# A graph layer on one core: edge tiles of 128 in blocks of 24, and a wait ahead of every eight gathers

## What is computed

```python
h = relu(layernorm(x))
m_in = concat([h[src], edge_attr])                    # 400000 x 192
messages = relu(m_in @ msg_w1 + msg_b1) @ msg_w2 + msg_b2
aggregated = segment_sum(messages, dst)               # 12500 x 128
out = x + relu(concat([h, aggregated]) @ upd_w1 + upd_b1) @ upd_w2 + upd_b2
```

## Time and profile before

| | |
|---|---|
| median of 3 runs | 4913.87 us (4913.0 to 4914.27) |
| profiled execution, own time | 4917.07 us |
| its span, first to last instruction | 4915.3 us |
| mean granted clock of TensorE | 0.608 of full speed |
| gathers, early and from the table | 75 and 3125 |

### The profile page before, as it was taken

How to read it: one execution, slowest core, us unless ns; L and a number is a source line. 1 busy time by engine, 2 the same in 40 slices (tenths; PEclk the granted TensorE clock), 3 DMA queues, 4 the chain that set the end, 5 groups by cost and what they waited for, 6 DMA issues and landing times.

```text
span 4915.3 us, 59369 instructions
## 1 busy us (share of the span) xinstructions
PE 3511.1 (71%) x16139; PEld 3183.0 (65%) x16139; DVE 2248.7 (46%) x3651; ACT 595.7 (12%) x887; POOL 3881.7 (79%) x3208
## 2 busy tenths in 40 slices
PE   5677777777677767766777677767776677767766
PEld 3666666666666666666666666666666666666666
DVE  5455555555444444444444444444444444444444
ACT  5111111111100000001010001000100010001002
POOL 7777777777778787877777777777777777777774
PEclk8666666666655555556555655655565655565566
DMA  7322222222222222222222222222222222222223
GB/s 174 73 67 64 69 66 67 68 66 67 64 64 64 65 65 64 64 64 64 64 66 64 64 64 65 64 64 64 65 65 64 64 64 66 64 64 64 65 64 87
DMA packets 398534, 336.04 MB, mean 68 GB/s; under 512 B 287275, under 2 KB 304299, under 8 KB 397263
## 3 DMA queue, kind: packets, MB, share of 16 engines
q0 software_dynamic: 256000, 208.52, 18.0%
q1 hardware_dynamic: 141810, 126.99, 10.5%
q10 hardware_dynamic: 706, 0.33, 0.0%
HBM read 319.26 MB, written 12.81 MB: 68 GB/s over the span
## 4 chain that ended last, share of the span: by engine, by line
POOL 72%; issue 23%; PE 2%; SPq 1%; DMA 1%; POOLq 0%; DVE 0%; another core or an unknown queue 0%; ACT 0%; ACTq 0%; DVEq 0%
POOL rows L380 72%; SPq L281 1%; PE pre L542 0%; POOLq L374 0%; PE seg L403 0%; DMA rows<-table,index 0%; PE pre L407 0%; PE pre L395 0%; POOLq L378 0%; DMA table<-space 0%; PE seg L467 0%; DMA b_upd_col<-in_b_upd 0%; DVE space L716 0%; PE iota_ps L542 0%
## 5 line engine op out<-in xcount | busy, mean ns | idle before, releaser
L380 POOL DMA_INDIRECT rows<-table,index x3125 | 3789.7, 1213 | 953.9 <-issue 953.0
L467 PE MATMUL seg<-space,hidden 125*128 125x128 f32 x6400 | 1517.1, 420 | 1030.1 <-ACT hidden L613 697.5
L467 PEld LDWEIGHTS seg<-space,hidden 125*128 125x128 f32 x6400 | 1353.0, 316 | 1166.2 <-issue 640.8
L785 DVE TENSOR_TENSOR hidden<-pre,rows 125x640 f32<-125x640 f32 x625 | 514.9, 824 | 1826.4 <-DMA rows<-table,index 1614.0
L433 PE MATMUL pre<-w_attr_sb,attr_space 64*125 64x128 f32 x6250 | 1304.0, 384 | 15.1 <-issue 15.1
L433 PEld LDWEIGHTS pre<-w_attr_sb,attr_space 64*125 64x125 f32 x6250 | 1173.1, 284 | 116.1 <-issue 103.7
L613 ACT ACTIVATE hidden<-hidden 125x640 f32<-125x640 f32 x640 | 471.5, 737 | 4247.4 <-DVE hidden L785 3476.0
L834 DVE TENSOR_REDUCE part_space<-space 125x128 f32<-125x640 f32 x640 | 790.6, 1235 | 0.0
L826 DVE TENSOR_TENSOR space<-iota_ps,dst_rel 125x640 f32<-125x640 f32 x640 | 526.0, 822 | 118.3 <-DVE part_space L834 71.1
L476 PE MATMUL seg<-part_space,w_msg_t_sb 128*128 128x128 f32 x1280 | 393.4, 407 | 224.8 <-DVE part_space L834 208.4
L476 PEld LDWEIGHTS seg<-part_space,w_msg_t_sb 128*128 128x128 f32 x1280 | 319.8, 306 | 258.7 <-issue 258.5
(11 more groups left out here) (65 smaller groups left out, 503.9 us busy)
## 6 DMA issues: line engine op xcount, KB each, us to landing
attr_space<-in_attr SPq DMA_DIRECT2D x640, 156.2 KB
rows<-table,index POOLq DMA_INDIRECT x3125
index<-in_src SPq DMA_DIRECT2D x625, 2.4 KB
table<-space SPq DMA_DIRECT2D x25, 224.0 KB
out<-x_all SPq DMA_DIRECT2D x4, 1120.0 KB
x_all<-in_x SPq DMA_DIRECT2D x2, 1120.0 KB
x_all<-in_x SPq DMA_DIRECT2D x1, 2240.0 KB
attr_space<-in_dst_rows SPq DMA_DIRECT2D x2, 781.2 KB
```

Of the source, the lines that this page charges most:

```text
L380: pool.indirect_dma_start(rows[0:EDGES, k, t, :], None, table, bass.IndirectOffsetOnAxis(index[:, k, t:t + 1], 0))\
L467: last = pe.matmul(seg[:, 0, 0:WINDOW], hidden[0:EDGES, hidden_slot(k), t * D:(t + 1) * D], mask[:, k % 2, t, :], start=(t == 0), stop=(t ...
L785: dve.tensor_tensor(hidden[0:EDGES, k, :], pre[0:EDGES, k % 2, 0:TILES * D], rows[0:EDGES, k].rearrange("p t d -> p (t d)"), ALU.add).then ...
```

## The change

The same computation with another cut of the edges and another order. New sizes:

```diff
-EDGES = 125
+EDGES = 128
 UNROLL = 5
-TILES = 5
-CHUNK = TILES * EDGES
-WINDOW = 128
+PAIR = 8
+PAIRS = 3
+TILES_B = PAIRS * PAIR
+SLOTS = 8
+AHEAD = 5
+WINDOW = 80
-EARLY = 15
+EARLY = 3
```

```diff
+            def gather(source, j, tiles):
+                for t in tiles:
+                    pool.indirect_dma_start(slot_rows(j)[:, t, :], None, source, bass.IndirectOffsetOnAxis(index[0:EDGES, j, t:t + 1], 0))\
+                        .then_inc(gathered[j][t // PAIR], 16)
...
+                need(pool, hidden_summed, b - (SLOTS - 1))
+                for q in range(pairs_of(b)):
+                    before_i, before_j, before_q = (i, j, q - 1) if q else (*behind(i, j, 1), PAIRS - 1)
+                    pool.wait_ge(gathered[before_j][before_q], before_i * (16 * PAIR) + 16 * PAIR)
+                    pool.sem_inc(pool_turns, 1)
+                    gather(table, j, range(q * PAIR, q * PAIR + tiles_of(b, q)))
```

- The attributes of two tiles stand one above the other on 128 partitions, and the weights are block-diagonal, so that one product of 256 columns serves two tiles:

```diff
-        w_attr_sb = sb("w_attr_sb", [2 * K_ATTR, D])
+        w_attr_sb = sb("w_attr_sb", [2 * K_ATTR, 2 * D])
...
+            def attr_product(i, j, q, two, stop):
+                start = q * COLUMNS + two * EDGES
+                return pe.matmul(columns(j, q, PAIR)[:, two * 2 * D:(two + 1) * 2 * D], attrs[:, j % 2, start:start + EDGES],
+                                 w_attr_sb[:, :], start=True, stop=stop)
```

More of the change, by code:

```diff
@@ L308, in _ @@
[L308 to L321, removed]
-                    sp.dma_start(attrs[:, k, :], attr[bass.ds(c, 1)].rearrange("a f e -> f (a e)"))\
-                        .then_inc(attr_loaded[k], 16)
@@ new lines, in load_block @@
+            def load_block(i, j):
+                b = block_of(i, j)
+                nxt = ahead(i, j, AHEAD)
+                if exists(*nxt) and not (isinstance(b, int) and b + AHEAD < SLOTS):
+                    need(sp, summed, b * PAIRS + (PAIRS - (SLOTS - AHEAD) * PAIRS))
+                    load_index(*nxt)
+                load_attr(i, j)
+            sp.wait_ge(update_ready, after(GROUPS - 1))
+            for j in range(SLOTS):
+                load_block(0, j)
+            with sp.Fori(1, ROUNDS) as i:
+                for j in range(SLOTS):
+                    load_block(i, j)
@@ L384, in _ @@
+            with pool.Fori(1, ROUNDS) as i:
+                for j in range(SLOTS):
+                    gather_block(i, j)
+            for i in range(ROUNDS, -(-(LAST + 1) // SLOTS)):
+                for j in rounds_of(i):
+                    gather_block(i, j)
         @block.tensor
@@ new lines, in update_sums @@
+            def update_sums(i, j):
+                if not exists(i, j):
+                    return
+                b = block_of(i, j)
+                width = pairs_of(b) * WINDOW
+                pe.wait_ge(part_copied, b + 1)
+                pe.wait_ge(mask_sums_made, b + 1)
+                need(pe, accumulated, b * PAIRS)
+                finished = sum(1 for at in FINISH.values() if isinstance(b, int) and at < b + (2 if b < LAST - 2 else 3))
+                need(pe, o_made, finished)
+                pe.matmul(spare[:, 0:width], w_both[:, :], part[:, j % 2, 0:width], start=True, stop=False)
+                pe.matmul(spare[:, 0:width], bias_both[0:EDGES, :], mask_sum[:, j % 2, 0:width], start=False, stop=True)\
+                    .then_inc(seg_ready, 1)
@@ new lines, in finish_group, with finish_groups @@
+            def finish_group(g):
+                pe.wait_ge(u_relued, g + 1)
+                need(pe, o_made, g)
+                for r in range(ROWS):
+                    last = pe.matmul(spare[0:NP, r * D:(r + 1) * D], u[:, r, :], w_upd2_sb[:, :], start=True, stop=True)
+                last.then_inc(o_ready, 1)
+            def finish_groups(i, j):
+                b = block_of(i, j)
+                for g, at in FINISH.items():
+                    if isinstance(b, int) and at == b:
+                        pe.wait_ge(accumulated, (b - 1) * PAIRS)
+                        finish_group(g)
@@ new lines, in edge_block @@
+            def edge_block(i, j, wide):
+                for q in range(pairs_of(block_of(i, j))):
+                    if wide:
+                        attr_products(i, j, q)
+                        wide_sums(i, j, q)
+                    else:
+                        nxt = (i, j, q + 2) if q == 0 else (*ahead(i, j), q - 1)
+                        if exists(*nxt) and nxt[2] < pairs_of(block_of(*nxt[:2])):
+                            attr_products(*nxt)
+                        if q == 0:
+                            update_sums(*behind(i, j, 2))
+                        hidden_sums(i, j, q)
+                if not wide:
+                    finish_groups(i, j)
@@ new lines, in copy_sums, with accumulate @@
+            def copy_sums(i, j):
+                if not exists(i, j):
+                    return
+                b = block_of(i, j)
+                width = pairs_of(b) * WINDOW
+                dve.wait_ge(hidden_summed, b + 1)
+                need(dve, seg_ready, b - 1)
+                dve.tensor_copy(part[:, j % 2, 0:width], seg[:, j % 2, 0:width]).then_inc(part_copied, 1)
+            sites = itertools.count()
+            def accumulate(i, j):
+                if not exists(i, j):
+                    return
+                b = block_of(i, j)
+                site = next(sites)
+                registers = [dve.alloc_register(f"base{c}_of_{site}") for c in range(pairs_of(b))]
+                dve.load(registers, base_row[0:1, bass.ds(b * BASES, pairs_of(b))])
+                for c in range(pairs_of(b)):
+                    base = bass.RuntimeValue.of_register_unchecked(registers[c], min_val=0, max_val=N - 1)
+                    if c == 0:
+                        dve.wait_ge(seg_ready, b + 1)
+                    need(dve, accumulated, b * PAIRS + c)
+                    place = update[:, bass.ds(base, WINDOW)]
+                    dve.tensor_tensor(place, spare[:, c * WINDOW:(c + 1) * WINDOW], place, ALU.add).then_inc(accumulated, 1)
@@ new lines, in edge_loops @@
+                one = divmod(LAST - 1, SLOTS)
+                two = divmod(LAST, SLOTS)
+                make_masks(*one)
+                for q in range(PAIRS):
+                    if q < PAIRS - 1:
+                        sum_rows(*one, q)
+                    if q == 0:
+                        sum_masks(*behind(*one, 1))
+                        copy_sums(*behind(*one, 1))
+                        accumulate(*behind(*one, 2))
+                    if q == 1:
+                        finish_groups(*one)
@@ new lines, in edge_loops @@
+                make_masks(*two)
+                sum_masks(*one)
+                sum_rows(*one, PAIRS - 1)
+                for q in range(PAIRS_LAST):
+                    sum_rows(*two, q)
+                accumulate(*behind(*one, 1))
+                copy_sums(*one)
+                sum_masks(*two)
+                copy_sums(*two)
+                accumulate(*one)
+                accumulate(*two)
+                dve.wait_ge(accumulated, LAST * PAIRS + PAIRS_LAST)
+                for g in REST:
+                    finish_group(g)
```

923 lines of the change are left out of this document (548 added, 375 removed).

## The result

The changed kernel took 4806.73 us (median of 4 runs, 4806.21 to 4807.37), beside 4914.07 for the kernel before: a ratio of 0.9782, with a 95% interval of [0.9765, 0.9799]. Forecast were 4682 us, a gain of 4.7%; measured were 2.2%. The profiled execution took 4807.37 us for a span of 4805.6.

What follows compares the result with a forecast made beforehand. Bound: the number of GpSimd gathers times their beat. Sum: 126 us start + 4530 for 381 groups of eight + 8 for the last five gathers + 19.5 tail = 4683 span, 4682 us as run time; range 4250 to 5550.

Steps and rivals of the forecast that it cites:

- Fewer, wider gathers: Gathers go from 3200 to 3125, 128 rows on 16 engines; descriptor pairs each from 416 to 144.
- g: A gather's work on GpSimd, 1.21 us before; taken as 1.00, bounds 0.50 and 1.24.
- Rival A: A gather's work on GpSimd stays at 1.21 us, so the kernel is slower, 5315 to 5545 us; chance 0.28.
- Rival D: A gather's work follows its descriptor pairs, 0.85 us or less, giving 4225 us; chance 0.20.
- D: Time from a gather's end on GpSimd to its landing, 2.15 us before; taken as 1.55.
- Rival C: The time from work's end to landing stays 2.15 us, giving 4911 us, no change; chance 0.07.
- r: Time from a landing to GpSimd's next gather start; taken as 0.17 us, upper end 0.90.
- Rival B: GpSimd restarts from idle, 0.90 us from landing to next start, giving 4960 us; chance 0.10.
- Rival E: GpSimd's wait costs nothing because the landing is already past, giving 4150 us; chance 0.03.
- The start: Early gathers and node stage ahead of the first table gather: 126 us, range 117 to 140.
- P: Cost of one group of eight table gathers including the wait for the eighth's landing: 11.89 us.
- The tail: From the last gather's landing to the end, with one output group left: 19.5 us, 45.2 before.

Runs made afterwards that it cites:

- run 1: The changed kernel without GpSimd's wait for the eight gathers before, all else kept: 3941.71 us, ratio 0.8015 against the kernel before.
- run 8: The changed kernel with the wait moved behind the first gather of each group: 4373.77 us, ratio 0.8899 against the kernel before.
- run 2: The kernel before with only the constant EDGES changed from 125 to 128 rows a gather, no wait: 3985.25 us, ratio 0.8102.
- run 6: The changed kernel with EDGES back at 125 rows a gather, wait and all else kept: 5962.18 us, ratio 1.2133 against the kernel before.
- run 3: The changed kernel with the wait kept, but for the group before the previous one: 3939.93 us, ratio 0.8012 against the kernel before.
- run 5: The changed kernel again, not edited, in two later jobs: 4734.48 and 4732.80 us, ratios 0.9634 and 0.963 against the kernel before.

## Why the prediction was right and where it was wrong

**The bound, right.** The kernel is still set by what one group of eight gathers costs on GpSimd; TensorE and VectorE stayed covered, busy for 52% and 30%, and even in run 1, for 62% and 37%. In run 8, where the chain is whole, it has 42% GpSimd, 32% issue and 23% DMA.

**Fewer, wider gathers, right.** 3125 gathers, 32 packets each. That these are 144 descriptor pairs on 16 engines remains an inference from the packets. The trace agrees on both shapes with the rule on the number of engines that the prediction quotes from the Trainium skill (DMA: Bandwidth & Descriptors, "Why a DMA increments its semaphore by 16 and not by 1"). Runs 2 and 6 switch between 32 and 80 packets by the constant alone.

**g, nearly right, and in part by luck.** Taken 1.00 (0.50 to 1.24), measured 0.944. The 1.00 was a choice between two bounds, not worked out from a row. That this term alone could turn the sign was true: Rival A, with 1.21, would have been slower, and run 6 measured such a kernel at +21%. Rival D, with g following the pairs (0.85 or less), fell. Only two shapes were measured, and they differ in rows, pairs and engines at once; which of these g follows isn't shown. One reading behind the split of 1.21 into 0.12 and 1.09 was too wide: in the kernel before, the L910 operations that began 0.05 us or more before a gather's start and ran on for 0.14 or more after it held it, but those that began from 0.02 before to 0.05 after it left it at 1.21, though they too covered its first 0.12.

**D, right.** Taken 1.55, measured 1.59; taking off the whole 0.60 of engine time was about right. With 125 rows the landing comes 3.33 - 1.21 = 2.12 after the work's end, close to the 2.15 of the earlier trace rows, so 0.53 were gained. Rival C, which kept 2.15, fell. A few single landings at 128 rows still took as long, this one 3.06 from the start:

```profile
4206.31 3.06 DMA rows<-table,index
```

The Trainium skill (DMA: Bandwidth & Descriptors, "Anatomy of one DMA") has a fixed part of about 2.0 us that scales with nothing. The traces do not agree with that: from start to landing a gather of 125 rows takes 3.33 us and one of 128 rows, with more bytes, 2.54.

**r, wrong.** This is the step that failed: "I take 0.17, from the loop that stays the loop". r measured 0.79, the size of Rival B's 0.90. The row behind the choice was misread. This is the timeline of the kernel before around it, and 14 us later:

```profile
795.84 1.21 POOL L380 DMA_INDIRECT rows<-table,index  x1 [0.30 <-issue]
797.36 1.21 POOL L380 DMA_INDIRECT rows<-table,index  x1 [0.30 <-DMA index<-in_src]
...
810.99 1.21 POOL L380 DMA_INDIRECT rows<-table,index  x1 [0.30 <-issue]
```

The index load landed at 797.19 and the queue's entry behind it followed at 797.21. But this is the 91st of 625 such entries, one ahead of each five gathers, so its own gather is the 451st from the table. Only 441 had started by then; the 451st is the one at 810.99. The gather at 797.36 had been issued before, and began after the usual 0.30 behind the one that ended at 797.05. So the 0.17 lies between two things that don't depend on each other: GpSimd's queue was nine gathers ahead here, and twelve at 497 of the 625 entries. The row at 126.08 was the only one with nothing queued, and its 0.88 was set aside as "code run for the first time". In terms of a group: the beats came out 0.43 lower than taken (7 x (1.31 - 1.248)), the last gather's work 0.06 lower, D 0.04 higher, r 0.62 to 0.65 higher: together the 0.20 between 12.09 and 11.89, or 77 us. The beats are lower because g is, so it was the error of g that hid much of the error of r: r alone is some 240 us (0.62 x 381). Rival B had r nearly right, and its 4960 was too high mostly because its g was 1.00. The prediction's own sign of being wrong came true, too: it named gaps of over 2.2 us ahead of every eighth gather, and they are 3.354 - 0.944 = 2.41, not 1.7. Of the 125 us by which the time was missed, the group has 77 and the start, below, 45.

**Rival E, wrong as a rival, right as a hint.** A wait that ends while gathers are still queued costs nothing: run 3. The prediction priced the wait well enough to be on the right side, but it reckoned the change as one sum. Taken apart, the change is a gain of some 975 us (run 1) and a loss of 793 (run 5 against run 1). Nothing that the runs show needs the wait where it stands. (The chances for a faster kernel add up to 0.585, not 0.57; nothing hangs on it.)

**The start, wrong for the recorded result, too cautious otherwise.** Forecast 126 (117 to 140), measured 171 there and 102 in both repeats, since the new node stage was done earlier. The shorter early gathers alone don't do it: in run 2, with the old node stage, they end at 98.05 and the first table gather starts at 124.97. With 102 and the measured P the sum is 4683 + 77 - 24 = 4736, against 4734 and 4733. The tail was nearly right: forecast 19.5 behind the last landing, measured 19.7 - 2.54 = 17.2.

## What to carry to other kernels

In this kernel GpSimd, waiting for the landing of what it had just issued, paid the landing and its own restart each time, 2.08 us; the same wait set one group back, with six gathers still queued when it ended, cost nothing. Price such a wait by a row in which the engine really stood still: if the idle time ahead of the row is the usual gap, the row says nothing about a restart. And before a landing is put beside the next start, count whether the two belong together; the chain of a profile joins what lies close in time. Before shapes are tuned, try the constants: of the 20% that were to be had here, 19 came from 128 rows a gather, a multiple of 16, in place of 125.

## What the hardware showed that was not expected

- GpSimd's work for an indirect gather of rows of 512 B was 1.21 us for 125 rows in 80 packets and 0.944 for 128 rows in 32 packets. More rows, less time.
- GpSimd's queue ran up to twelve gathers ahead of GpSimd where no wait held it (at 368 of 382 entries in run 1, 497 of 625 in the kernel before), and was six ahead at most entries in run 3.
- After a wait that ends with nothing queued, GpSimd's next gather begins 0.79 us after the landing (0.93 with 125 rows, 1.09 in run 8), while the gap between two queued gathers is 0.30 in every run. In run 8 the 1.09 is the same whether the landing came 0.14 or 2.97 us after the end of GpSimd's work.
- The node stage of one program took 70 us longer in one job than in two others, with the steps of several engines each 15 to 36 us late and the DMA engines idle for four fifths of the stretch from 50 to 100 us. No run here explains it.
